# First tile, projections, last outputs and output projection around a serial recurrence, rebuilt over several banks and buffers

## The reference

```python
x = x + attn_a(layernorm(x))        # segment-wise softmax attention, 16 heads
x = x + ffn(layernorm(x))           # ternary weights, 256 -> 1024 -> 256, rms norms, gelu
x = x + attn_b(layernorm(x))        # the recurrence below
x = x + ffn(layernorm(x))
```

```python
sa = state @ (-kk_t)
state = w_t * state + sa x (kk_t * a_t) + k_t x v_t      # x: outer product, 16 x 16 per head
state = state / (sqrt(mean(state**2, -1)) + 1e-5)
o_t = sum(state * r_t[..., None], -1)
```

## Time and profile before

| | |
|---|---|
| median of 3 executions | 2524.98 us (2518.33 to 2525.3) |
| the profiled execution | 2528.14 us, span 2526.2 us |
| PE busy, weight loads | 1928.5 us (76%), 1550.7 us (61%) |
| DVE busy | 2188.2 us (87%) |
| ACT busy | 1597.9 us (63%) |
| POOL busy | 893.6 us (35%) |
| mean granted TensorE clock | 0.814 of full |

### The profile page before, as it was taken

How to read it: one execution, slowest core, us unless ns; L and a number is a source line. 1 busy time by engine, 2 the same in 40 slices (tenths; PEclk the granted TensorE clock), 3 DMA queues, 4 the chain that set the end, 5 groups by cost and what they waited for, 6 DMA issues and landing times. The chain is left out here.

```text
span 2526.2 us, 48033 instructions
## 1 busy us (share of the span) xinstructions
PE 1928.5 (76%) x12353; PEld 1550.7 (61%) x12353; DVE 2188.2 (87%) x8801; ACT 1597.9 (63%) x5207; POOL 893.6 (35%) x1522
## 2 busy tenths in 40 slices
PE   5888888788688777778888877778887784435687
PEld 3555555455487767777777777667777774433455
DVE  5888886688409999999999999999999999993687
ACT  4788887577446665556666666666666555443576
POOL 0000000010005555555555555555555555551110
PEclk7899999699887787777777778997776775666799
DMA  5000010000000000000000000000000000000001
GB/s 177 17 21 17 17 32 13 1 1 1 1 1 1 2 1 1 1 1 1 1 1 1 1 1 1 1 1 1 1 1 1 1 1 1 1 1 1 1 27 41
DMA packets 14354, 25.03 MB, mean 10 GB/s; under 512 B 1280, under 2 KB 12032, under 8 KB 13824
## 3 DMA queue, kind: packets, MB, share of 16 engines
q1 hardware_dynamic: 14080, 21.97, 3.0%
HBM read 12.27 MB, written 4.19 MB: 7 GB/s over the span
## 5 line engine op out<-in xcount | busy, mean ns | idle before, releaser
L1590 POOL TENSOR_TENSOR wu<-U,stg 128x256 f32<-128x256 f32 x512 | 318.2, 622 | 682.3 <-DVE U L1513 682.3
L712 PE MATMUL bank<-U,ident 128*128 128x128 f32 x2080 | 469.2, 397 | 95.6 <-ACT go L974 79.3
L712 PEld LDWEIGHTS bank<-U,ident 128*128 128x128 f32 x2080 | 432.5, 238 | 132.6 <-issue 97.1
L775 PE MATMUL bank<-stack,tm 128*128 128x64 f32 x1792 | 326.6, 366 | 174.5 <-ACT tm L911 174.5
L1113 ACT ACTIVATE xs<-U 128x128 f32<-128x128 f32 x1024 | 260.9, 302 | 279.4 <-DVE U L1513 276.0
L775 PEld LDWEIGHTS bank<-stack,tm 128*128 128x128 f32 x1792 | 315.2, 276 | 193.8 <-ACT tm L911 193.8
L1456 DVE TENSOR_REDUCE pn<-xs 128x16 f32<-128x256 f32 x1024 | 378.3, 410 | 0.3
L1546 POOL TENSOR_TENSOR kv<-stg 128x256 f32<-128x256 f32 x513 | 318.1, 620 | 0.0
L1041 ACT ACTIVATE small<-pn 128x16 f32<-128x16 f32 x513 | 110.9, 216 | 295.5 <-DVE pn L1456 295.5
L1472 DVE TENSOR_TENSOR bank<-wu,bank 128x128 f32<-128x128 f32 x1024 | 293.6, 287 | 1.3 <-POOL wu L1590 0.8
L697 PE MATMUL bank<-wcat,yT 128*128 128x224 f32 x1024 | 287.9, 439 | 1.7 <-issue 1.7
(11 more groups left out here) (180 smaller groups left out, 3588.4 us busy)
## 6 DMA issues: line engine op xcount, KB each, us to landing
out_x<-x SPq DMA_DIRECT2D x8, 512.0 KB, 2.9
x<-in_x SPq DMA_DIRECT2D x1, 3584.0 KB, 17.0
Vs<-V SPq DMA_DIRECT2D x8, 384.0 KB, 4.7
Vs<-V SPq DMA_DIRECT2D x8, 288.0 KB, 3.3
lane<-in_lanes SPq DMA_DIRECT2D x8, 256.0 KB, 3.3
wcat<-in_wcat SPq DMA_DIRECT2D x1, 1792.0 KB, 14.3
wraw<-in_w_up SPq DMA_DIRECT2D x1, 1024.0 KB, 19.1
wraw<-in_w_down SPq DMA_DIRECT2D x1, 1024.0 KB, 11.4
```

Source lines behind the costliest of these rows:

```text
L712: last = pe.matmul(rsum.rearrange("p (t i) -> p t i", i=HD), ident[:, :], steps[:, :, :, j], start=(j == 0), stop=(j == HD - 1))
L775: last = pe.matmul(bank[3 + g][:, e * CH:(e + 1) * CH], tm[:, g * (PB // 2) + e, :, :].rearrange("p a c -> p (a c)"), stack[:, :], start=T ...
L1590: pool.tensor_tensor(ij(wu[:, :]), ij(U[:, half if j else 1 - half, (j - 1) % STEPS, :]), col(stg[:, half, j, TW, :]), ALU.mult).then_inc( ...
```

## The change

Ahead of the recurrence:

- Scale and shift of the first tile of each batch item (`tile_columns`) are computed inside the first FFN (q = 3 and q = 5), by GpSimd's power of -0.5 in place of ACT's root and DVE's reciprocal. Those of the other three tiles (`other_columns`) follow after the FFN, beside the first tile. DVE's clear of tm is the first clear; R is moved to another place in SBUF, y has two buffers.
- The first tile: ACT normalises item m into y[m % 2] and copies the features of item m - 1 from bank 3 + (m - 1) % 3 straight to yT. Its convolution is left out here and done in chunk n = 1 (`convolved`, `TURN`) from a buffer yTz that ACT fills from yT.
- The projections of group m alternate between banks 1, 2 and 6, 7 (`projected`), and PE projects m before it turns m - 1 (`turn_pairs`).

Behind the recurrence:

- DVE sums the last eight states with two reductions (`last_row_sums`) in place of PE's 32 instructions and ACT's copy.
- ACT copies all outputs in two instructions to `ovs_all` (the memory of tm), PE turns 16 columns into banks 4 to 7, ACT and DVE copy two banks each to go. ACT loads the gelu table here.
- The second FFN's first rows (statistics, roots, normalisation, turn, halves) stand before the output loop.
- The output loop: PE turns go itself into bank 2 + m % 2, ACT copies to one of two buffers, PE multiplies by Wo into bank 4 + m % 4, ACT squares; GpSimd takes the root for two items at a time, DVE scales and adds.

The core of the diff (helpers of the FFN are moved out unchanged as `turned_rows`, `high_half`, `low_half`, `row_roots`):

```diff
+            for m in range(B):
+                pe.wait_ge(C["yn"], m + 1)
+                pe.wait_ge(C["yd"], max(m - 2, 0))
+                for k in range(KD):
+                    last = pe.transpose(bank[3 + m % 3][:, k * P:(k + 1) * P], y[:, m % 2, k * P:(k + 1) * P], ident[:, :])
+                last.then_inc(C["yt"], 1)
+            pe.wait_ge(C["yd"], B)
+            for m in range(NB + 1):
+                if m == 1:
+                    pe.wait_ge(F["x"], B * NT)
+                if m < NB:
+                    project(-1, m, 0)
+                    project(-1, m, 1)
+                if m >= 1:
+                    turn_pairs(-1, m - 1)
...
+            def turn_pairs(n, m):
+                i = beside(n)[1] * NB + m
+                pe.wait_ge(C["ev"], i * 4 + 4)
+                pe.wait_ge(C["rc"], i * 2)
...
+            act.wait_ge(C["nm"], 1)
+            for m in range(B + 1):
+                if m < B:
+                    normalise_first(m)
+                if m >= 1:
+                    features_first(m - 1)
+            act.preload_act_table_set("natural_log_exp_and_others")
+            act.wait_ge(ld_w, NLW)
+            act.wait_ge(C["tz"], 1)
+            for m in range(NB + 1):
+                if m < NB:
+                    evacuate_projection(-1, m, 0)
+                    evacuate_projection(-1, m, 1)
+                if m >= 1:
+                    evacuate_pairs(-1, m - 1, 0)
+                    evacuate_pairs(-1, m - 1, 1)
...
+        def convolved(n):
+            return {0: 1, 1: 0, 2: 2, 4: 3}.get(n)
...
+            for m in range(NB):
+                pe.wait_ge(Z["os"], m // 4 + 1)
+                for e in range(2):
+                    c = (m % 2 * 2 + e) * P
+                    last = pe.matmul(bank[4 + m // 2][CH:2 * CH, c:c + P], ovs_all[:, 2 * m + e, :], ident[:, :],
+                                     start=True, stop=True, skip_group_check=True)
+                last.then_inc(Z["t1"], 1)
+            for k in (1, 0):
+                turned_rows(pe, B, k)
+            pe.wait_ge(Z["goa"], 2)
+            pe.wait_ge(Z["god"], 2)
+            for m in range(B + 1):
+                if m < B:
+                    pe.wait_ge(Z["gc"], max(m - 1, 0))
+                    for k in range(KD):
+                        last = pe.transpose(bank[2 + m % 2][:, k * P:(k + 1) * P], go[:, 1, m, k * P:(k + 1) * P], ident[:, :])
+                    last.then_inc(Z["gt"], 1)
+                if m >= 1:
+                    pe.wait_ge(Z["gc"], m)
+                    if m >= 5:
+                        pe.wait_ge(Z["sq"], m - 4)
+                        pe.wait_ge(O["t"], (NT - 1) * B + m - 4)
+                    for k in range(KD):
+                        last = pe.matmul(bank[4 + (m - 1) % 4][:, 0:D], goT_pair[(m - 1) % 2][:, k, :], wo_b[:, k, :],
+                                         start=(k == 0), stop=(k == KD - 1))
+                    last.then_inc(Z["pr"], 1)
...
+            last_row_sums(0)
+            dve.wait_ge(S["rt"], L + 1)
+            dve.tensor_scalar(sring[:, 3, :], rt, LN_EPS, None, ALU.add).then_inc(S["sg"], 1)
+            dve.wait_ge(S["sg"], L + 1)
+            dve.tensor_copy(hist[:, 1, RENORM:, :], sring).then_inc(S["h"], 1)
+            last_row_sums(4)
+            row_stats(dve, B)
+            row_moments(dve, B)
+            row_scales(dve, B)
+            rows_normalised(dve, B, range(NT))
+            dve.wait_ge(O["gs"], (NT - 1) * B)
+            for c in (1, 3):
+                dve.wait_ge(Z["t1"], 2 * c + 2)
+                dve.tensor_copy(four_rows(c), four_sums(c)).then_inc(Z["god"], 1)
+            row_stats(dve, B + 1)
+            row_moments(dve, B + 1)
+            for k in (1, 0):
+                low_half(dve, B, k)
+            for pair in range(B // 2):
+                two = slice(2 * pair, 2 * pair + 2)
+                dve.wait_ge(Z["rt"], pair + 1)
+                dve.tensor_scalar(oss[:, 2, two], oss[:, 1, two], D ** -0.5, 1e-6, ALU.mult, ALU.add).then_inc(Z["dn"], 1)
+                dve.wait_ge(Z["dn"], pair + 1)
+                dve.reciprocal(oss[:, 2, two], oss[:, 2, two]).then_inc(Z["iv"], 1)
...
```

More of the change, by code:

```diff
@@ L440, in ffn_dve, with ffn_pool @@
                 next_moments(q9)
[L442 to L445 removed]
+        def ffn_pool(pool, i):
             def output_roots(q):
@@ new lines, in _ @@
+            root(L + 1)
+            log_norms(L // STEPS, 1, L // RENORM + 1)
+            factors(L // STEPS, 1)
+            act.wait_ge(O["ov"], L // STEPS + 1)
+            for part in range(2):
+                i8 = slice(part * HD // 2, (part + 1) * HD // 2)
+                act.activation(ovs_all[:, i8, :], ov[:, CH:2 * CH, i8].rearrange("p t i -> p i t"), ACT.Copy).then_inc(Z["os"], 1)
+            act.preload_act_table_set("gelu_and_others")
+            for c in (0, 2):
+                act.wait_ge(Z["t1"], 2 * c + 2)
+                act.activation(four_rows(c), four_sums(c), ACT.Copy).then_inc(Z["goa"], 1)
@@ new lines, in _ @@
+            for k in (1, 0):
+                high_half(act, B, k)
+            for m in range(B + 1):
+                if m < B:
+                    act.wait_ge(Z["gt"], m + 1)
+                    act.wait_ge(Z["pr"], max(m - 1, 0))
+                    act.activation(goT_pair[m % 2], bank[2 + m % 2][:, 0:D].rearrange("p (k t) -> p k t", t=P),
+                                   ACT.Copy).then_inc(Z["gc"], 1)
+                if m >= 1:
+                    act.wait_ge(Z["pr"], m)
+                    act.wait_ge(Z["sq"], max(m - 2, 0))
+                    act.activation((osq, y[:, 0, :].rearrange("p (k t) -> p k t", t=P))[m % 2], bank[4 + (m - 1) % 4][:, 0:D].rearrange("p (k t) -> p k t", t=P), ACT.Square,
+                                   accum_out=oss[:, 0, m - 1:m]).then_inc(Z["sq"], 1)
@@ new lines, in _ @@
+            for e in range(2):
+                dve.wait_ge(T[e]["u"], L)
+            last_row_sums(0)
[8 more added lines that the diff above has]
+            rows_normalised(dve, B, range(NT))
@@ L1617, in _ @@
             outputs(L // STEPS, L % (2 * CH) + 2 * CH - STEPS)
-            ffn_pool(pool, 1, False)
+            row_roots(pool, B)
+            row_roots(pool, B + 1)
+            for pair in range(B // 2):
+                two = slice(2 * pair, 2 * pair + 2)
+                pool.wait_ge(Z["sq"], 2 * pair + 2)
+                pool.tensor_tensor(oss[:, 1, two], oss[:, 0, two], halves[:, 0, 0:2], ALU.pow).then_inc(Z["rt"], 1)
+            ffn_pool(pool, 1)
 def constants():
```

400 lines of the change are left out of this document (214 added, 186 removed).

## The result

The median of the changed kernel is 2435.72 us (2434.98 to 2441.28, four runs) against 2525.14 for the kernel before (2518.33 to 2527.68, four runs): a ratio of 0.9668, interval 0.9645 to 0.9691. The forecast was 2448, range 2436 to 2470. The profiled execution took 2441.28 us with a span of 2439.2; before, 2528.14 and 2526.2.

What follows compares the result with a forecast made beforehand. The prediction took VectorE to bound the recurrence, with waiting chains of 114 us ahead and 77 us behind. Gains of 34.9 - 2.8 - 0.35 - 0.2 + 45 = 76.5 us took 2524.98 to 2448 us, range 2436 to 2470.

Steps and rivals of the forecast that it cites:

- the cover of the convolution's additions: Recurrence, chunk 1: eight VectorE additions lie in a wait it has anyway; 0.2 us lost, up to 3.4 if uncovered.
- tm's one buffer and ScalarE's six copies: Projections: six ScalarE copies between two turns keep the cycle at 7.58 us against 7.61; nothing expected per group.
- the low clock: Projections: two groups again run at a lowered TensorE clock, 6.3 us, making the stretch 71.9 us.
- The second pair of banks: Projections, rival: it closes TensorE's gap, groups 6.6 us, seven times 1.0 less, 2441 us in all; chance 0.08.
- (a): Behind the recurrence: two VectorE reductions of about 1.2 us replace TensorE's 7.28 us row sums; product ends at 2297.7.
- (b): Behind the recurrence: two ScalarE output copies of 1.0 us, then eight pairs of turns in 7.5 us, to 2306.2.
- (c): Behind the recurrence: eight transposes of the second FFN's first rows, 1.2 us, to 2307.4; Wo(0) starts at 2309.3.
- (d): Output loop: TensorE is slowest at 1.5 us per batch item with hand-overs; Wo runs from 2309.3 to 2321.0.
- (e): After the output loop: square, power, small ones and two 0.9 us VectorE steps until its first hidden tile, 2324.6.
- the rival on the clock: Behind the recurrence, TensorE stays at half clock: 11 us more, 2459, or 2478 with all projection groups; chance 0.18.
- the first tile waited for nothing: First tile, negated rival: it waits after all, up to 20 us; 2458 with half, 2468 with all; chance 0.05.
- no step got 0.15 us longer: Recurrence, negated rival: each of 512 steps gets longer; 0.15 us decides, 0.2 us gives 2550 us; chance 0.03.

Runs made afterwards that it cites:

- e4: Changed kernel with everything behind the recurrence as before the change, everything ahead of it as changed: 2486.72 us, ratio 0.9856.
- e3: Changed kernel with the projections alone back in the old order and over one pair of banks: 2436.42 us, ratio 0.9659.
- e2: Changed kernel with ScalarE's first R copy ahead of the four tm copies, each half turn waiting for its own bank's copy: 2426.33 us, ratio 0.962.
- e6: Changed kernel with the last eight row sums back on TensorE: span 2436.3 us, 31.03 us from last states to second FFN.
- e7: Changed kernel with the second FFN's first rows behind the output loop again: span 2444.0 us, 38.06 us from last states to second FFN.
- e8: Changed kernel with TensorE turning each output item only after the previous item's Wo: span 2437.3 us, 31.43 us from last states to second FFN.
- e10: e2 with VectorE's output additions for the last two batches behind the second FFN's first two hidden tiles: 2424.59 us, ratio 0.9605.
- e11: e10 with an extra identity transpose on TensorE behind the first tile's turns, into an unread bank: 2421.64 us, ratio 0.9604.
- e9: Changed kernel with five identity transposes in TensorE's gap ahead of each turn of the projections: 2436.82 us, ratio 0.9659.
- e5: Changed kernel with the first tile's convolution left out altogether, so chunk 1 lacks its matmuls, copy and additions: 2445.78 us, one time.

## Why the prediction was right, and where its sizes were off

The direction and the mechanisms held, but for the cover of the convolution's additions. The median of 2435.72 lies 0.3 us below the range; the ratio applied to the 2524.98 that the forecast started from gives 2441.2, inside it. That the median came out at the edge is in part the sizes and in part the head: the forecast of 76.5 us gained stands against 82.7 by the marks, and the 4.35 us of the head come on top.

**First tile** (34.9 forecast, 36.4 measured). The path was as told: ScalarE sets the pace, and neither TensorE's turn nor VectorE's clears show. What was mis-sized is "0.97 a tile with a small overlap". On ScalarE the copy of 0.38 begins 0.11 before the normalisation of 0.60 ends, and the next normalisation 0.11 before that copy ends; a tile costs 0.76. No run took the pieces of this part (the clears, the table load, the buffers) apart; e4 shows it and the projections together.

**Projections** (2.8 lost forecast, 3.9 measured). The step that counted, that tm's one buffer and ScalarE's six copies leave the cycle as it was, held: 7.45 against the 7.58 of the sum, since two R copies in a row take 1.67 and not 1.88. The pause of 1.08 us ends with the R copy, as foretold, and e3 shows that the new order bought nothing. What was too small is the low clock, taken as two groups or 6.3 us: it struck in three of seven turns' distances, 5.0 us, but also in the last turn, which waits 4.16 us and then runs at the lower clock each time (6.21 and not 3.34). The fill took 8.7 and not 8.2. By the distances: 8.7 + 57.1 + 6.2 + 1.1 = 73.0 as measured, where the forecast's terms made 71.9. How often the clock falls between the first turn and the last is the execution's: B was 67.8 to 73.1 in the seven executions with this same order of work.

**The second pair of banks** was rightly held to close nothing, but the forecast missed something beside it. The forecast's text names the wait on the R copies beside tm as evidence against a closed gap; it did not ask whether that wait is needed in that place. It was not: e2 changes no buffer, only one wait and the place of one copy, and TensorE runs through at 6.15 a group.

**Additions in the first FFN** (0.35 lost forecast, 0.1 measured). The head moves by up to 9 us between executions, but the FFN in it does not: from ScalarE's first square to the end of its last it takes 151.7 us before and 151.8 after.

**Recurrence** (0.2 lost forecast, 0.73 measured). Within what the forecast allowed for a shift (-1 to +4.5), but not by the mechanism. The step that the additions lie in a wait that VectorE has anyway was half right: in chunk 1 VectorE works 1.71 us more and idles 0.87 less, 0.84 lost. That chunks 1 and 2 agreed before does not show such a wait, since chunks move by more than that for no work of their own: chunk 0, with as many VectorE instructions as before, is 1.8 longer, and later ones are shorter. That C lost only 0.73 is in part such moves that cancel.

**Behind the recurrence** (45 forecast, 51.8 measured). This was the largest miss, all in one direction. From the last small reduction to the first hidden tile the forecast's terms are 30.4 and the trace has 24.9, from 2258.1 to 2282.97:

| term | forecast | measured |
|---|---|---|
| (a) reductions, factors, product | 3.5 | 3.2 |
| (b) copies and turns, to the last sum | 8.5 | 7.0 |
| (c) to the first Wo | 3.1 | 2.0 |
| (d) first Wo to the end of the last | 11.7 | 8.9 |
| (e) to VectorE's first hidden tile | 3.6 | 3.7 |

In (b) the turns took 5.8 and not 7.5. Windows of the changed kernel in them, one early and one late (the figure behind x counts every matmul that lies in the window, if only in part; the last but two is the granted clock):

```profile
2265.00:2266.00 1.00, 1.00 (x6) 1.00 (x5) 0.96 (x4) 0.73 (x1) 0.00 (x0) 0.50 0.00 0
2267.00:2268.00 1.00, 1.00 (x12) 1.00 (x11) 0.54 (x1) 0.50 (x1) 0.00 (x0) 1.00 0.00 0
```

At half clock the trace starts one every 0.213 us, for the first 4.3 us, and the last eleven at full clock every 0.109. The forecast took 0.28 at half clock from a block of four that stands alone (1.11). Each of these matmuls lasts 0.42 in the trace, beyond the start of the next: a row's duration holds the end of its last one, which a dense block pays once. All 32 at half clock would be 7.0 (an estimate, 31 x 0.213 and 0.42), not 8.9, and the clock gave 1.2 back. The same slip stands in the rival on the clock: 0.23 each for the 32 row sums was read as a clock that had risen, but they start 0.217 apart both in their first 3.5 us, at a granted clock of 0.55, and behind that, at 1.00. In (d) "TensorE is the slowest at 1.5 with hand-overs" is wrong: 0.38 and 1.03 to 1.17 lie partly over one another and there is no hand-over left to pay, since the turn goes ahead; 1.12 a batch item. And the 1.3 us taken off "for eight hand-overs that I may have missed" were not missed. 5.5 + 1.3 = 6.8 is the whole difference. The second FFN, costed at nothing with up to 1 us to come back, lost 0.9: TensorE idles 2.73 us for VectorE's late start. e4 confirms the whole part by itself, e6, e7 and e8 three of its pieces: 5.0, 12.0 and 5.4 us of 51.8.

The forecast of the head's gain, 34.9 - 2.8 = 32.1, against 32.5 measured, looks better than it is: two errors of 1.5 and 1.1 us cancel. Of the rivals none came: the groups were never 6.6 apart, the clock was back 4.3 us into the tail's turns, the first tile waited for nothing, and no step got 0.15 us longer.

## What to carry to other kernels

When an engine pauses once a round, read which semaphore its wait counts, and then the order in which the engine that raises it does its work; another pair of banks moved the pause from one copy to another, and moving one copy ahead of four others removed it. A serial stretch in front of or behind a full loop is worth as much as its length, and its pieces can be priced one by one if the marks are taken inside the trace, where they repeat to a tenth of a microsecond while whole times scatter by several. An engine that is late at the end of a shortened tail gives a part back in the next stage, and moving its work past the border (e10) only moves the wait if that engine has no slack there.

## What the runs showed of the hardware that was not expected

- The granted clock fell in stretches in which TensorE was busy for 8.9 of 10 us: to 0.67 between 690 and 700 us in the changed kernel, in three of the seven distances there, but in one or two in the same code in e6 to e8, and for a shorter time. In the three runs in which TensorE never paused between its projections (e2, e10, e11) the groups stayed 6.15 us apart. That the pause pulls the clock down fits this but is not shown; e9 with its smaller pause could not tell it from chance.
- After one longer pause it fell each time. Ahead of the second FFN's first down product TensorE idled 2.63 to 2.73 us in eight executions, and the clock fell in or just behind that product in all of them; with 1.26 and 1.92 us (e10, e11) it stayed up. The last turn, behind 4.16 us of idle time, took 6.20 or 6.21 us in all eight executions with that order.
- Independent instructions in a row on ScalarE and TensorE cost less than the sum of their durations: 0.76 us for 0.60 + 0.38, 1.67 for two of 0.94, 6.15 for 3.25 + 3.23.
- VectorE's 1024 instructions for the new state, of 0.28 us each, had 2.0 us of idle time before them that no other engine ends in the kernel before, 2.8 in the changed kernel and in ten of the eleven others, and 4.0 in e5. It is the same in each execution of one kernel and another after an edit elsewhere. VectorE's whole idle time in the recurrence need not follow it: 5.41, 5.2 to 5.3, and 7.56.
- A power on GpSimd costs by the elements of a partition: 0.70 us for two, 1.01 for four, 1.67 for eight, 4.16 for 24.
